# Expert slots walked backwards, and partial tiles filled with the expert's own rows in place of written padding rows

## The chip, the cores and the metric

One core of one Trainium2 chip runs the whole kernel in one launch. The metric is the device time of that execution in microseconds. The kernel before takes 541.59 us (median of 3 runs, 537.69 to 542.88). Engine names are those of the profile: PE (TensorE matmul), PEld (its weight loads), DVE (VectorE), ACT (ScalarE), POOL (GpSimd), SP (SyncE); a "q" behind an engine's name (SPq) marks what its instruction queue does by itself, above all the issue of a DMA.

## The reference

128 images of 64x64 give 16 patches each, 2048 tokens of 192 numbers:

```
h = patches @ W.T + b                                   # 768 -> 192
h = h + attention(layernorm(h))                         # 12 heads, 16 tokens of an image, causal, rotary
x = layernorm(h); t = rmsnorm(x) * norm_scale
g = t @ gate_w.T + gate_b                               # 16 experts
top_vals, top_idx = top_k(g, 4); w = softmax(top_vals)
y_e = swiglu(t @ mlp1_w[e].T + mlp1_b[e]) @ mlp2_w[e].T + mlp2_b[e]   # 192 -> 768 -> 384 -> 192
out = h + x + sum over the 4 chosen experts of w_e * y_e
```

Only the four chosen experts of a token count, so 8192 (token, expert) rows have to be computed. Routing by the reference on its own inputs gives experts 0 to 15 these numbers of rows: 361, 358, 1251, 439, 850, 869, 271, 312, 448, 426, 436, 688, 708, 72, 644, 59. In tiles of 128 rows that is 3, 3, 10, 4, 7, 7, 3, 3, 4, 4, 4, 6, 6, 1, 6 and 1: 72 tiles.

## The kernel before, in words

**Stage one** handles 16 tiles of 128 tokens in a software pipeline of seven steps: embedding, attention, norms, gate, top 4, and the place of each chosen row in the DRAM table `routed`. Each expert owns a region of `routed`; `scatter` (L1133) sends a tile's rows with four indirect DMAs from POOL, one for each choice. A routed row (`packet`, 212 numbers) holds the token's 192 values, its 16 weights and its token number. `add_bias` (L982) completes the residual `base`, which SP stores to `out` (`store_base`, L359).

**Between the stages** three things have to be ready. (a) Padding: `pad_regions` (L316) writes, for each expert, 128 rows of zeros (with a token number below the output) behind the expert's last row, 8 experts from SP, 6 from ACT and 2 from POOL; it knows where from `fill_i` (L1004), which exists only once the last tile is counted. (b) The slot table: 16 small DVE steps, each of which waits for the one before (`then_wait`, L1037), give for each of the 79 slots its expert, its first row in `routed`, and the scatter it must wait for (`owed`); PE turns three columns (L557) and DVE copies them to `table_i` (L1070). (c) All 64 scatters have landed. SP waits for all of it (L384 to L389) before it loads the first tile of rows (L396).

**Stage two** runs 79 slots, the most that 16 experts can need; slot j is one tile of one expert. PE, ACT and DVE take slots in pairs: PE turns the rows (L574), multiplies by the first layer (L594, L602), later by the second (L616); ACT copies weights (L639), applies silu (L730) and notes the row weight (L747); DVE adds the bias, clips, multiplies (L1077, L1082, L1090), and `weigh` (L1093) multiplies by the row weight into one of NY = 4 buffers `y_out` (L1097), where it waits for the scatter of slot j-4. POOL adds the tile to `out` with an indirect DMA that accumulates (L1196). Two such DMAs may touch the same token if they belong to different experts. So POOL always waits for scatter j-2 (L1187), and for scatter j-1 (L1194) where the table says so: where slot j is the first tile of an expert, and for every slot past the last used tile. Those spare slots read a region of padding rows and compute like any other. In the kernel before, the used tiles are slots 0 to 71 in the order of the experts, and the spare ones are slots 72 to 78.

The changed lines, whole:

Of the kernel before, what the change touches and what calls it, by code (L numbers as in the profile page):

```python
# [16 lines left out]
P = 128  # L17
# [23 lines left out]
PAD_SPLIT = (0, 8, 14, 16)  # L41
TABLE_STEPS = 16
# [18 lines left out]
for _name, _n in (("ident", P), ("cos", HD), ("sin", HD), ("head", HH), ("odd", 2), ("own", 2), ("causal", SEQ),  # L61
                  ("expert", EXPERTS), ("region", EXPERTS), ("grow", EXPERTS), ("tile", 1), ("pad", 1),
                  ("before", P), ("token", TILES), ("owed", 1)):
    C_COLS[_name] = (_at, _at + _n)
    _at += _n
# [3 lines left out]
def shape_constants():  # L69
# [3 lines left out]
    def put(name, value):  # L73
        a, b = C_COLS[name]
        c[:, a:b] = value
# [22 lines left out]
def build(nc, x, consts, w_tok, b_tok, w_qkv, b_qkv, w_proj, nscale, w_gate, b_gate,  # L98
          w1, b1, w2, b2, out):
    routed = nc.dram_tensor("routed_rows", (SPARE + P, ROW), F32, kind="Internal").ap()  # L100
    with ExitStack() as ctx:
# [33 lines left out]
        pad_row = sb("pad_row", [P, ROW])  # L135
# [44 lines left out]
        cnt = sb("cnt", [P, EXPERTS])  # L180
        cnt_i, cnt_i2 = sb("cnt_i", [P, EXPERTS], I32), sb("cnt_i2", [P, EXPERTS], I32)
        fill_i = sb("fill_i", [1, EXPERTS], I32)
        ntile, tend = sb("ntile", [P, EXPERTS]), sb("tend", [P, EXPERTS])
        passed, jump, jumped = sb("passed", [P, EXPERTS]), sb("jump", [P, EXPERTS]), sb("jumped", [P, EXPERTS])
        of_tile = sb("of_tile", [P, 6])
        passed_n = sb("passed_n", [P, EXPERTS])
# [15 lines left out]
        row_w = sb("row_w", [P, NX])  # L202

# [10 lines left out]
        def turned(b, a, rows=HALF):  # L214
# [10 lines left out]
        ps_tab = banks[3][0:1, 0:3 * SLOTS]  # L225
# [11 lines left out]
        setup_pool, setup_dve, setup_act, pad_done = sem("setup_pool"), sem("setup_dve"), sem("setup_act"), sem("pad_done")  # L237
# [13 lines left out]
        counted, table_step, fill_ready, table_turned, table_ready, spare_out = (  # L251
            sem(n) for n in ("counted", "table_step", "fill_ready", "table_turned", "table_ready", "spare_out"))
        pads_out = [sem(f"pads_out{i}") for i in range(3)]
# [3 lines left out]
                   "experts_done y_out_ready").split()  # L257
# [58 lines left out]
        def pad_regions(eng, i):  # L316

            eng.wait_ge(fill_ready, 1)
            with eng.Fori(PAD_SPLIT[i], PAD_SPLIT[i + 1] - 1, 2) as e0:
                for u in range(2):  # L320
                    at = eng.value_load(fill_i[0:1, bass.ds(e0 + u, 1)], min_val=0, max_val=SPARE - P)  # L321
                    eng.dma_start(routed[bass.ds(at, P), :], pad_row[:]).then_inc(pads_out[i], 16)  # L322

# [4 lines left out]
        def _(sp):  # L328
# [47 lines left out]
            sp.wait_ge(pad_done, 1)  # L376
            sp.dma_start(routed[SPARE:SPARE + P, :], pad_row[:]).then_inc(spare_out, 16)
            sp.dma_start(out[TOKENS:TOKENS + P, :], pad_row[:, 0:DIM]).then_inc(dump_out, 16)
# [5 lines left out]
            sp.wait_ge(spare_out, 16)  # L384
            for i in range(3):
                sp.wait_ge(pads_out[i], 16 * (PAD_SPLIT[i + 1] - PAD_SPLIT[i]))
# [24 lines left out]
        def _(pe):  # L411
# [142 lines left out]
            pe.wait_ge(s["base_full"], TILES)  # L554
            pe.wait_ge(table_step, TABLE_STEPS)
            for i in range(3):
                last = mm(ps_tab[:, i * SLOTS:(i + 1) * SLOTS], of_tile[0:SLOTS, i:i + 1], ident[0:SLOTS, 0:SLOTS],  # L557
                          start=True, stop=True)
            last.then_inc(table_turned, 1)
# [6 lines left out]
            pe.wait_ge(s["base_full"], TILES)  # L566
            pe.wait_ge(s["row_i_ready"], TILES)
# [69 lines left out]
        def _(act):  # L637
# [78 lines left out]
            pad_regions(act, 1)  # L716
# [54 lines left out]
        def _(dve):  # L771
# [6 lines left out]
            V.tensor_copy(pad_row[:, ID_AT:ID_AT + 1].bitcast(I32), const("pad")).then_inc(pad_done, 1)  # L778
# [183 lines left out]
            def place_all(t):  # L962
                dve.wait_ge(s["ranked"], t + 1)
                V.tensor_tensor(place[:], ps_r, const("region"), ALU.add).then_inc(s["place_ready"], 1)
# [23 lines left out]
            def step(tile, seen, n):  # L988
# [12 lines left out]
                if isinstance(tile(6), int) and tile(6) == TILES - 1:  # L1001

                    dve.wait_ge(counted, 1)
                    V.tensor_tensor(fill_i[:], ps_cnt[0:1, :], const("region", 1), ALU.add).then_inc(fill_ready, 1)  # L1004
# [25 lines left out]
                at(6, add_bias)  # L1030
# [6 lines left out]
            def then_wait(instruction):  # L1037

                instruction.then_inc(table_step, 1)
                made[0] += 1  # L1040
                dve.wait_ge(table_step, made[0])


            then_wait(V.tensor_scalar(cnt_i[:], ps_cnt, float(P - 1), None, ALU.add))
            then_wait(V.tensor_scalar(cnt_i2[:], cnt_i[:], P.bit_length() - 1, None, ALU.logical_shift_right))
            then_wait(V.tensor_copy(ntile[:], cnt_i2[:]))
            then_wait(V.tensor_tensor_scan(tend[:], ones_f[:], ntile[:], 0.0, ALU.mult, ALU.add))

            then_wait(V.tensor_scalar(jump[:], ntile[:], -float(P), float(REGION), ALU.mult, ALU.add))

            then_wait(V.tensor_scalar(passed[:], tend[:], const("tile"), None, ALU.is_le))
            then_wait(V.tensor_tensor(jumped[:], passed[:], jump[:], ALU.mult))
            then_wait(V.tensor_reduce(of_tile[:, 2:3], passed[:], AX_X, ALU.add))
# [201 lines left out]
```

## Time and profile before

| | |
|---|---|
| median of 3 runs | 541.59 us (537.69 to 542.88) |
| profiled execution | 542.0 us, span 540.2 us |
| PE / ACT / DVE / POOL busy | 440.9 / 310.8 / 298.8 / 256.9 us |
| chain that ended last, by engine | PE 57%, issue 9%, DVE 9%, ACT 6%, DMA 4%, SPq 4%, POOL 4% |
| L594 PE, first layer, 948 matmuls | 124.0 us |
| L616 PE, second layer, 474 matmuls | 83.9 us |
| L1196 POOL, 25 of the 79 accumulating scatters | 40.1 us, 1605 ns each |
| L1140 POOL, 64 scatters into `routed` | 63.5 us, 992 ns each |

The span has three parts. Stage one fills it up to some 220 us, then there is a stretch in which PE hardly works, then stage two. Shares of busy time over the whole span mix these, so the rows further down are read stretch by stretch. A timeline row gives start, duration, engine, line, operation and, in brackets, how long the engine had been idle before and what released it; a group such as "x8" spans from its first to its last member.

### The profile page before, as it was taken

Reading aid. Unit: us, or ns where it says so; the run is one execution under the profiler, and the core shown is the slowest. Engines: PE = TensorE matmul, PEld = TensorE weight load, DVE = VectorE, ACT = ScalarE, POOL = GpSimd, SP = SyncE. Lnnn points to the kernel's source line nnn. Section 1 sums busy time; section 2 is a strip of 40 time slices with the busy share of each in tenths; the row PEclk is TensorE's granted clock in tenths of the full one; section 3 lists DMA queues with packets and bytes.
Section 4 is the critical chain, followed back from the end, with each engine's and each line's share of the span. In section 5 each row is a group of like instructions: output and inputs, shape, how many; then the busy total and the mean of one; then the engine's idle time right before and its main releaser. Section 6 shows DMA issues by size and latency. Waiting matters only on the chain.

```text
span 540.2 us, 14340 instructions
## 1 busy us (share of the span) xinstructions
PE 440.9 (82%) x3865; PEld 390.1 (72%) x3866; DVE 298.8 (55%) x964; ACT 310.8 (58%) x832; POOL 256.9 (48%) x303
## 2 busy tenths in 40 slices
PE   2888977878787767119999999999999999999910
PEld 2676756556665545108999999999999999999910
DVE  0467968878778665403555555555555555555510
ACT  1247656666556642016777777777777777777600
POOL 1114576667677556700346444444444444444332
PEclk9789999999997755558999999999999999999965
DMA  8965454565541111333234444444344444432211
GB/s 222 257 158 166 138 152 147 172 172 153 153 134 51 41 41 56 128 114 101 52 55 78 61 63 61 63 61 61 53 69 61 61 61 62 63 40 30 24 22 22
DMA packets 41914, 49.72 MB, mean 92 GB/s; under 512 B 6387, under 2 KB 33251, under 8 KB 41860
## 3 DMA queue, kind: packets, MB, share of 16 engines
q1 hardware_dynamic: 26452, 33.48, 23.1%
q0 software_dynamic: 14544, 14.94, 17.9%
q10 hardware_dynamic: 864, 0.65, 0.4%
q8 instruction: 25, 0.41, 0.3%
q14 instruction: 29, 0.24, 0.2%
HBM read 30.82 MB, written 18.23 MB: 91 GB/s over the span
## 4 chain that ended last, share of the span: by engine, by line
PE 57%; issue 9%; DVE 9%; ACT 6%; another core or an unknown queue 5%; DMA 4%; SPq 4%; POOL 4%; POOLq 1%; DVEq 0%; ACTq 0%
PE bank L594 21%; PE bank L616 14%; PE bank L602 11%; PE bank L574 3%; PE bank L422 2%; ACT k_spread L657 2%; ACT p_spread L639 2%; POOL routed_rows L1140 2%; DMA out_rows<-x_sb 1%; SPq L322 1%; DMA x_sb<-patches 1%; SPq L321 1%; DVE t_row L902 1%; POOL rstd L1131 1%
## 5 line engine op out<-in xcount | busy, mean ns | idle before, releaser
L594 PE MATMUL bank<-rT,w_now 128*128 128x128 f32 x948 | 124.0, 281 | 0.3 <-ACT rT L639 0.3
L594 PEld LDWEIGHTS bank<-rT,w_now 128*128 128x128 f32 x948 | 115.1, 193 | 5.2 <-ACT rT L639 0.5
L730 ACT ACTIVATE k_spread<-bank,w_now 128x128 f32<-128x128 f32 x237 | 69.9, 372 | 58.1 <-PE bank L602 58.1
L1077 DVE TENSOR_TENSOR v_sb<-bank,w_now 128x384 f32<-128x384 f32 x79 | 44.1, 558 | 101.4 <-PE bank L602 80.4
L639 ACT ACTIVATE w_now<-w_sb 128x1158 f32 x79 | 92.5, 1171 | 13.4 <-issue 7.9
L616 PE MATMUL bank<-w_sb,p_spread 128*128 x474 | 83.9, 327 | 0.1
L1196 POOL DMA_INDIRECT out_rows<-x_sb,wtok_sb x25 | 40.1, 1605 | 79.9 <-issue 33.0
L616 PEld LDWEIGHTS bank<-w_sb,p_spread 128*128 128x128 f32 x474 | 76.1, 190 | 0.5 <-issue 0.4
L1140 POOL DMA_INDIRECT routed_rows<-packet,row_i x64 | 63.5, 992 | 24.2 <-issue 22.5
L602 PE MATMUL bank<-rT,w_now 64*128 64x128 f32 x948 | 64.2, 282 | 0.0
L1090 DVE SCALAR_TENSOR_TENSOR p_spread<-k_spread,v_sb 128x384 f32<-128x384 f32 x79 | 44.2, 560 | 35.7 <-ACT k_spread L730 31.4
L602 PEld LDWEIGHTS bank<-rT,w_now 64*128 64x128 f32 x948 | 56.4, 188 | 5.0 <-issue 0.2
L422 PE MATMUL bank<-wtok_sb,x_sb 128*128 128x192 f32 x192 | 38.5, 356 | 10.0 <-DMA wtok_sb<-w_tok 5.7
L422 PEld LDWEIGHTS bank<-wtok_sb,x_sb 128*128 128x128 f32 x192 | 36.0, 212 | 10.0 <-DMA wtok_sb<-w_tok 5.3
L657 ACT ACTIVATE k_spread<-bank,cst 96x256 f32<-96x256 f32 x96 | 36.4, 480 | 0.0
L639 ACT ACTIVATE p_spread<-pT 32x384 f32<-32x384 f32 x64 | 33.2, 518 | 2.6 <-DVE pT L872 2.0
L639 ACT ACTIVATE rT<-bank 128x256 f32<-128x256 f32 x79 | 26.2, 381 | 13.7 <-PE bank L574 13.0
L1097 DVE TENSOR_SCALAR x_sb<-bank,row_w 128x192 f32<-128x192 f32 x79 | 29.2, 410 | 5.4 <-DMA out_rows<-x_sb,rope_s 3.9
L639 ACT ACTIVATE yT<-bank 128x384 f32<-128x384 f32 x16 | 7.8, 490 | 40.1 <-remote 37.3
L1082 DVE TENSOR_SCALAR v_sb<-v_sb 128x384 f32<-128x384 f32 x79 | 29.2, 369 | 2.7
L467 PE MATMUL bank<-wproj_sb,yT 128*128 128x192 f32 x96 | 23.1, 386 | 8.1 <-issue 4.4
L1128 POOL TENSOR_SCALAR ve<-mv 128x1 f32<-128x1 f32 x32 | 7.2, 225 | 44.2 <-DVE mv L802 36.1
(174 smaller groups left out, 688.6 us busy)
## 6 DMA issues: line engine op xcount, KB each, us to landing
x_sb<-patches SPq DMA_DIRECT2D x16, 384.0 KB, 3.4
w_sb<-w SPq DMA_DIRECT2D x32, 192.0 KB
w_sb<-w SPq DMA_DIRECT2D x16, 288.0 KB
w_sb<-w SPq DMA_DIRECT2D x64, 48.0 KB
wtok_sb<-routed_rows SPq DMA_DIRECT2D x25, 106.0 KB, 2.0
out_rows<-h SPq DMA_DIRECT2D x16, 96.0 KB
wproj_sb<-routed_rows SPq DMA_DIRECT2D x10, 106.0 KB
x_sb<-routed_rows SPq DMA_DIRECT2D x10, 106.0 KB
```

What stands on the lines that cost most here:

```text
L422: last = mm(ps_e, x_sb[buf][:, c, :], wtok_sb[:, c, :], start=(c == 0), stop=(c == PCH - 1))
L594: last = mm(dst[:, c * P:(c + 1) * P], w[:, a:a + P], t[:, part, :], start=(start and c == 0), stop=(not start and c == ICH - 1))
L602: last = mm(dst[:, c * P:(c + 1) * P], w[k:k + half, REST + c * P:REST + (c + 1) * P], t[k:k + half, 1 - part, :], start=(start and c == 0 ...
L616: last = mm(ps_yo[buf % 2], act_sb[buf % 4][:, c, :], w2_sb[:, bass.ds(expert, 1), c, :].rearrange("p a f -> p (a f)"), start=(c == 0), st ...
L639: return nc.scalar.activation(dst, src, ACT.Copy)
L657: last = nc.scalar.activation(k_spread[:, :, :, h], ps_kT.rearrange("p c (j i k) -> p c j i k", j=PAIRS, i=2), ACT.Copy, scale=const("head ...
L730: last = nc.scalar.activation(gate_act[b][:, a:a + P], ps_glu[b][:, a:a + P], ACT.Silu, bias=w1_now[b][:, GLU_B + c:GLU_B + c + 1], scale= ...
L1077: V.tensor_tensor(lin[b].rearrange("p (c t) -> p c t", c=ICH), ps_lin[b][:, 0:INNER].rearrange("p (c t) -> p c t", c=ICH), w1_now[b][:, LI ...
L1082: V.tensor_scalar(lin[b], lin[b], 1.0 + LIMIT, 1.0 - LIMIT, ALU.min, ALU.max).then_inc(r["clip_ready"], 1)
L1090: V.scalar_tensor_tensor(act_sb[buf % 4].rearrange("p c t -> p (c t)"), gate_act[b], SILU_LIMIT, lin[b], ALU.min, ALU.mult).then_inc(r["ac ...
L1140: G.indirect_dma_start(out=routed, out_offset=bass.IndirectOffsetOnAxis(ap=row_i[buf][:, k:k + 1].bitcast(U32), axis=0), in_=packet[buf][: ...
L1196: G.indirect_dma_start(out=out, out_offset=bass.IndirectOffsetOnAxis(ap=rows[b][:, ID_AT:ID_AT + 1].bitcast(U32), axis=0), in_=y_out[b % N ...
```

## The change

Slot j now takes tile 78-j of the old order: `tile` becomes 78 minus the slot, so the spare slots are 0 to 6 and the last slots are the tiles of expert 0. Within an expert too the last tile comes first. No padding is written behind an expert's rows. A slot whose tile is partial starts at (last row - 127) and so reads the last 128 rows of its expert; the rows that a neighbouring slot owns too are computed twice, and their results are sent to the 128 rows below the output. For that each region begins with 128 rows of zeros (needed by an expert with fewer than 128 rows), written by SP ahead of the routing's end: 17 DMAs. In stage two DVE makes the list of target rows (`row_to`) for each slot with one more instruction on 128x1 elements, POOL waits for it, and the scatter uses it. `owed` is set where a slot is its expert's last tile, and for spare slots. The table needs 22 steps where 16 stood, each of which waits only for the step it reads; the last `add_bias` runs behind them; a fourth matmul and one DVE instruction make `pad_to`, the list of double rows.

```
-PAD_SPLIT = (0, 8, 14, 16)
-TABLE_STEPS = 16
+TABLE_STEPS = 22
...
-    put("region", np.arange(EXPERTS)[None, :] * REGION)
+    put("region", np.arange(EXPERTS)[None, :] * REGION + P)
-    put("tile", p[:, None])
+    put("tile", SLOTS - 1 - p[:, None])
+    put("next", SLOTS - p[:, None])
+    put("past", -P * (SLOTS - 1 - p[:, None]))
+    put("row", P - p[:, None])
...
-        def pad_regions(eng, i):
-            eng.wait_ge(fill_ready, 1)
-            with eng.Fori(PAD_SPLIT[i], PAD_SPLIT[i + 1] - 1, 2) as e0:
...
-            sp.wait_ge(pad_done, 1)
-            sp.dma_start(routed[SPARE:SPARE + P, :], pad_row[:]).then_inc(spare_out, 16)
+            sp.wait_ge(setup_pool, 3)
+            sp.dma_start(out[TOKENS:TOKENS + P, :], zero_row[:, 0:DIM]).then_inc(dump_out, 16)
+            for e in range(EXPERTS + 1):
+                sp.dma_start(routed[e * REGION:e * REGION + P, :], zero_row[:]).then_inc(heads_out, 16)
-            with sp.Fori(TILES - 8, TILES - 1) as t:
+            with sp.Fori(TILES - 8, TILES) as t:
                 store_base(t)
-            pad_regions(sp, 0)
-            store_base(TILES - 1)
+            sp.wait_ge(heads_out, 16 * (EXPERTS + 1))
...
+            mm(ps_valid, of_tile[0:SLOTS, 3:4].to_broadcast([SLOTS, P]), ident[0:SLOTS, 0:SLOTS],
+               start=True, stop=True).then_inc(table_turned, 1)
+            pe.wait_ge(pad_to_ready, 1)
+            pe.wait_ge(setup_dve, 4)
...
-            pad_regions(act, 1)
...
+            tab(10, V.tensor_reduce, column[7], ends_at[:], AX_X, ALU.max)
+            tab(15, V.scalar_tensor_tensor, column[3], column[6], cnt[:, 0:1], const("past"), ALU.add, ALU.add)
+            tab(16, V.tensor_tensor, column[9], column[7], passed[:, EXPERTS - 1:EXPERTS], ALU.max)
+            tab(19, V.scalar_tensor_tensor, column[1], column[3], float(P), column[8], ALU.min, ALU.add)
+            tab(20, V.scalar_tensor_tensor, column[2], column[9], 16.0, const("owed"), ALU.mult, ALU.add)
+            add_bias(TILES - 1)
+            dve.wait_ge(table_turned, 1)
+            V.tensor_copy(table_i[:].rearrange("p a j -> p (a j)"), ps_tab).then_inc(table_ready, 1)
+            V.tensor_scalar(pad_to[:], ps_valid, const("row"), const("pad"), ALU.is_lt, ALU.mult)
...
             def weigh(j, buf):
+                V.scalar_tensor_tensor(row_to[:, buf % NY:buf % NY + 1], rows[buf][:, ID_AT:ID_AT + 1].bitcast(I32),
+                                       float(TOKENS - 1), pad_to[:, bass.ds(j, 1)], ALU.min, ALU.max)
...
-            pad_regions(pool, 2)
...
+                    pool.wait_ge(r["row_to_ready"], j + 1)
-                        ap=rows[b][:, ID_AT:ID_AT + 1].bitcast(U32), axis=0),
+                        ap=row_to[:, b % NY:b % NY + 1].bitcast(U32), axis=0),
```

How the change moves instructions shows at two places. First SP, from the store of the zero rows below the output to the first load of routed rows; before:

```order
L377 DMA routed_rows<-pad_row 128x212 [waits pad_done]
L378 DMA out_rows<-pad_row 128x192
L361 DMA out_rows<-h 128x192
...
L319 UNCONDITIONAL_BRANCH [waits fill_ready]
L321 TENSOR_LOAD fill_i
L322 DMA routed_rows<-pad_row 128x212
...
L361 DMA out_rows<-h 128x192 [waits base_full]
L395 TENSOR_LOAD table_i [waits scattered0,scattered1,pads_out2,table_ready,pads_out1,spare_out,pads_out0]
L396 DMA wtok_sb<-routed_rows 128x212
```

and now:

```order
L372 DMA out_rows<-zero_row 128x192 [waits setup_pool]
L374 DMA routed_rows<-zero_row 128x212 x17
L356 ISA [waits base_full]
...
L387 TENSOR_LOAD table_i [waits table_ready,scattered1,heads_out,scattered0]
L388 DMA wtok_sb<-routed_rows 128x212
```

The padding loop behind the last count is gone, and 17 DMAs stand far ahead of it. Second DVE, from the last placing of rows to the table's copy (`cnt_i`, `of_tile` and the like are the table's workings, `w_sb` the first layer's bias columns); before:

```order
L980 CAST row_i<-row_f 128x4 [waits scattered1,row_f_ready]
L986 TENSOR_TENSOR h<-h,bank 128x192 [waits base_ready,b2_done]
L1044 TENSOR_SCALAR cnt_i<-bank 128x16
...
L1063 SCALAR_TENSOR_TENSOR of_tile<-of_tile,cst 128x1 [waits table_step]
L1067 TENSOR_SCALAR w_sb<-bank 128x16x3 [waits b1_turned,table_step]
L1068 TENSOR_SCALAR w_sb<-bank 128x16x3
L1070 CAST table_i<-bank 1x237 [waits table_turned]
```

and now:

```order
L975 CAST row_i<-row_f 128x4 [waits scattered1,row_f_ready]
L1033 TENSOR_SCALAR cnt_i<-bank 128x16 [waits counted]
L1033 COPY cnt<-bank 128x16
...
L1033 SCALAR_TENSOR_TENSOR of_tile<-of_tile,cst 128x1 [waits table_step]
L981 TENSOR_TENSOR h<-h,bank 128x192 [waits base_ready,b2_done]
L1063 CAST table_i<-bank 1x237 [waits table_turned]
L1064 TENSOR_SCALAR pad_to<-bank,cst 128x79
L1068 TENSOR_SCALAR w_sb<-bank 128x16x3 [waits b1_turned]
L1069 TENSOR_SCALAR w_sb<-bank 128x16x3
```

The residual's last addition has moved behind the table's steps, and the bias columns behind the table's copy.

## Rows read from the trace of the kernel before

**Rows 1.** The page: PE's busy tenths in 40 slices of 13.5 us.

```profile
PE   2888977878787767119999999999999999999910
```

**Rows 2.** Timeline between the stages, all engines: start us, us, engine, line, idle before.

```profile
217.50 0.96 POOL L1140 DMA_INDIRECT routed_rows<-packet,row_i  x1 [0.30 <-issue]
...
219.98 0.36 ACT L639 ACTIVATE packet<-t_row 128x192 f32<-128x192 f32 x1 [2.88 <-DMA routed_rows<-packet,row_i]
...
220.92 0.17 DVE L980 CAST row_i<-row_f 128x4 int32<-128x4 f32 x1
...
221.93 0.17 DVE L1044 TENSOR_SCALAR cnt_i<-bank 128x16 int32<-128x16 f32 x1
...
222.84 15.71 SPq L322 DMA_DIRECT2D routed_rows<-pad_row  x8
...
224.53 0.15 DVE L1058 TENSOR_SCALAR of_tile<-of_tile 128x1 f32<-128x1 f32 x1
225.01 0.17 DVE L1059 TENSOR_TENSOR passed_n<-passed,ntile 128x16 f32<-128x16 f32 x1 [0.33 <-issue]
...
227.62 0.96 POOL L1140 DMA_INDIRECT routed_rows<-packet,row_i  x1 [0.30 <-issue]
227.83 0.16 DVE L1063 SCALAR_TENSOR_TENSOR of_tile<-of_tile,cst 128x1 f32<-128x1 f32 x1 [0.48 <-DVE of_tile L1061]
...
229.34 0.95 PE L557 MATMUL bank<-cst,of_tile 79*1 79x79 f32 x6 [7.72 <-DVE of_tile L1063]
...
231.00 0.38 DVE L1070 CAST table_i<-bank 1x237 int32<-1x237 f32 x1
...
242.79 0.66 PE L574 MATMUL bank<-cst,wtok_sb 128*128 128x128 f32 x2 [12.15 <-DMA wtok_sb<-routed_rows]
```

**Rows 3.** Timeline of SP's queue: before stage one ends, and the first row loads.

```profile
154.98 0.43 SPq L378 DMA_DIRECT2D out_rows<-pad_row  x1
161.34 56.52 SPq L361 DMA_DIRECT2D out_rows<-h  x7
...
240.69 3.64 SPq L396 DMA_DIRECT2D wtok_sb<-routed_rows  x4
```

**Rows 4.** The chain that ended last, in order of time: start us, us, what.

```profile
238.22 1.69 DMA routed_rows<-pad_row
...
263.26 1.95 PE bank L616 x12
...
494.46 1.95 PE bank L616 x12
```

**Rows 5.** Timeline of POOL in stage two: its scatters into the output.

```profile
259.64 1.66 POOL L1196 DMA_INDIRECT out_rows<-x_sb,wtok_sb  x1 [29.91 <-DVE x_sb L1097]
...
272.69 1.54 POOL L1196 DMA_INDIRECT out_rows<-x_sb,wtok_sb  x1 [2.77 <-DVE x_sb L1097]
...
301.30 1.56 POOL L1196 DMA_INDIRECT out_rows<-x_sb  x1 [3.79 <-issue]
303.17 1.55 POOL L1196 DMA_INDIRECT out_rows<-x_sb  x1 [0.30 <-issue]
...
506.73 1.72 POOL L1196 DMA_INDIRECT out_rows<-x_sb,p_pair  x1 [2.68 <-DMA out_rows<-x_sb,pT]
511.86 1.55 POOL L1196 DMA_INDIRECT out_rows<-x_sb,rope_c  x1 [3.41 <-DMA out_rows<-x_sb,p_pair]
...
533.00 1.56 POOL L1196 DMA_INDIRECT out_rows<-x_sb,k_spread  x1 [2.59 <-DMA out_rows<-x_sb]
```

**Rows 6.** Timeline of DVE in stage two: a pair in the middle, and the last ones.

```profile
299.17 0.74 DVE L1097 TENSOR_SCALAR x_sb<-bank,row_w 128x192 f32<-128x192 f32 x2
301.55 0.56 DVE L1077 TENSOR_TENSOR v_sb<-bank,w_now 128x384 f32<-128x384 f32 x1 [1.64 <-PE bank L602]
...
503.07 0.73 DVE L1097 TENSOR_SCALAR x_sb<-bank,row_w 128x192 f32<-128x192 f32 x2
...
515.51 0.42 DVE L1097 TENSOR_SCALAR x_sb<-bank,row_w 128x192 f32<-128x192 f32 x1 [1.51 <-PE bank L616]
519.85 0.42 DVE L1097 TENSOR_SCALAR x_sb<-bank,row_w 128x192 f32<-128x192 f32 x1 [3.92 <-DMA out_rows<-x_sb,rope_s]
```

More of the change, by code:

```diff
@@ L61 @@
 for _name, _n in (("ident", P), ("cos", HD), ("sin", HD), ("head", HH), ("odd", 2), ("own", 2), ("causal", SEQ),
-                  ("expert", EXPERTS), ("region", EXPERTS), ("grow", EXPERTS), ("tile", 1), ("pad", 1),
+                  ("expert", EXPERTS), ("region", EXPERTS), ("grow", EXPERTS), ("tile", 1), ("next", 1), ("past", 1), ("row", 1), ("pad", 1),
                   ("before", P), ("token", TILES), ("owed", 1)):
@@ L1029, in step, with tab @@
                 at(1, rope_add)
-                at(6, add_bias)
+                if n < TILES + STAGES - 2:
+                    at(6, add_bias)
             unrolled(STAGES, TILES, step)
             made = [0]
-            def then_wait(instruction):
-                instruction.then_inc(table_step, 1)
+            def tab(needs, op, *args):
+                if needs:
+                    dve.wait_ge(table_step, needs)
+                op(*args).then_inc(table_step, 1)
                 made[0] += 1
-                dve.wait_ge(table_step, made[0])
@@ L1044, in _ @@
[L1044 to L1051, printed above, removed]
@@ L1064, in _ @@
-            assert made[0] == TABLE_STEPS
+            column = [of_tile[:, i:i + 1] for i in range(10)]
+            dve.wait_ge(counted, 1)
+            tab(0, V.tensor_scalar, cnt_i[:], ps_cnt, float(P - 1), None, ALU.add)
+            tab(0, V.tensor_copy, cnt[:, 0:EXPERTS], ps_cnt)
+            tab(1, V.tensor_scalar, cnt_i2[:], cnt_i[:], P.bit_length() - 1, None, ALU.logical_shift_right)
+            tab(2, V.tensor_tensor, fewer[:], cnt[:, 1:EXPERTS + 1], cnt[:, 0:EXPERTS], ALU.subtract)
@@ new lines, in _ @@
+            tab(3, V.tensor_copy, ntile[:], cnt_i2[:])
+            tab(5, V.tensor_tensor_scan, tend[:], ones_f[:], ntile[:], 0.0, ALU.mult, ALU.add)
+            tab(5, V.tensor_scalar, jump[:], ntile[:], -float(P), float(REGION), ALU.mult, ALU.add)
+            tab(5, V.scalar_tensor_tensor, left[:], ntile[:], float(P), fewer[:], ALU.mult, ALU.add)
+            tab(6, V.tensor_scalar, passed[:], tend[:], const("tile"), None, ALU.is_le)
+            tab(6, V.tensor_scalar, ends_at[:], tend[:], const("next"), None, ALU.is_equal)
@@ L1065, in _ @@
+            assert made[0] == TABLE_STEPS
+            add_bias(TILES - 1)
+            dve.wait_ge(table_turned, 1)
+            V.tensor_copy(table_i[:].rearrange("p a j -> p (a j)"), ps_tab).then_inc(table_ready, 1)
+            V.tensor_scalar(pad_to[:], ps_valid, const("row"), const("pad"), ALU.is_lt, ALU.mult
+                            ).then_inc(pad_to_ready, 1)
             dve.wait_ge(b1_turned, 1)
```

70 lines of the change are left out of this document (29 added, 41 removed).

## The prediction, written before the changed kernel ran

> **What bounds the kernel now.** I read the page's busy slices first: PE is busy at 90% or more from slice 20 on, and works at a tenth in slices 17 and 18 [rows 1]. So stage two is PE's, and two stretches are not: the gap between the stages and the end. The timelines of these two and the chain that ended last say what each waits for.
>
> Stage two in its middle: the chain is PE alone, and a pair of slots takes (494.46 - 263.26) / 34 = 6.80 us [rows 4], 3.40 a slot. DVE is idle for 1.64 us before it starts a pair [rows 6]. POOL issues a pair's two scatters at 301.30 and 303.17, 2.13 us after DVE began to weigh the pair at 299.17, and 1.87 apart [rows 5, 6].
>
> The gap: the last scatter into `routed` is issued at 227.62; the table is in place at 231.38 (231.00 + 0.38) [rows 2]. Yet SP issues its first row load at 240.69 [rows 3]. The chain shows why: it passes through a padding DMA that lands at 239.91 (238.22 + 1.69) [rows 4]; SP's eight padding DMAs alone stretch over 15.71 us [rows 2]. PE starts 2.10 us after that load, at 242.79, having been idle for 12.15 us.
>
> The end: the last slot is weighed at 519.85, after 3.92 us of waiting for a free `y_out` buffer, and POOL issues the last six scatters from 511.86 to 533.00, (533.00 - 511.86) / 5 = 4.23 us apart, each released by the landing of the one before [rows 5, 6]. Those are slots 73 to 78, all spare. A chained scatter takes 4.2 us where PE needs 3.4 for the slot, so at the end of the program POOL runs long after PE, for rows that nobody reads.
>
> **The change, part by part.**
>
> *Padding leaves the gap.* SP now waits for the later of two things. The scatters: the last of an earlier tile was issued at 217.50 and released ACT at 219.98, so it lands 2.48 us after its start; the last one of all, started at 227.62, lands at 230.1 [rows 2]. POOL's own queue of scatters sets this, and the change leaves it alone. The table: DVE can start at 221.1, behind the cast at 220.92 (+0.17); `add_bias`, which stood ahead and waited for PE, is behind the table now. The first twelve steps took from 221.93 to 224.68, 0.23 us each; the last four from 225.01 to 227.99, 0.75 each, while padding DMAs were in flight [rows 2]. I have 22 steps: at 0.23 they end at 226.2. With slow steps like those four at 0.75 it is 228.2, and with every step behind 225.0 at 0.75 (five of them) 228.8. Then PE: 1.35 us from step to matmul (227.99 to 229.34), 0.95 for three transposes and a third of that, 0.32, for the fourth, and 0.1 + 0.38 for the copy: 3.1 us, with 0.35 for `add_bias` hidden beside PE. Table in place: 229.3, at worst 231.9. SP's first load came 0.78 us behind the last padding (240.69 against 239.91), so now at 230.9 if the scatters decide and at 232.7 if the worst table does. I take 231.4, half a microsecond above the lower end, since slow steps have been seen once: **9.3 us less**, between 8.0 and 9.8. What would be late next: PE also waits for the bias columns and `pad_to`, three small DVE instructions behind the copy, about 0.9 us; the rows need 2.1 us from issue to PE, so these hide. ACT's table load and first weight copy stood behind its padding loop and now run ahead.
>
> A rule of the Trainium skill ("SBUF — State Buffer", the part on the "DVE blocks DMA" trap) speaks against the longer table: while VectorE runs certain fp32 instructions it locks GpSimd out of the port through which it writes DMA descriptors. By that rule the six added steps, 0.17 us each, could put up to 1.0 us on the last scatter's landing and on the sum. The trace speaks for none: the scatters from 217.50 to 227.62 are (227.62 - 217.50) / 8 = 1.265 us apart, with table steps beside some of them and an idle DVE beside others [rows 2].
>
> *17 zero DMAs from SP.* They follow the store at 154.98, at 0.47 us each: 8 us, to about 163. SP's next job, a store, waited until 161.34 anyway [rows 3], so it slips by some 2 us and nobody waits for it. On the DMA engines they run beside stage one's last expert weights and the scatters of three or four tiles. I cost this at nothing: a packet buffer is reused two tiles later. If that cover were gone, the bound is the padding's own length, some 16 us for 8 on SP with others beside [rows 2]; stage one's 22 pipeline steps in 220 us are 10 us each, so two of them still cover it, and I allow 3 us for what shares the queues beside. A gain has no reason.
>
> *Reversal, the start.* Slots 0 to 6 are spare, 7 is expert 15's only tile, 8 expert 14's last: scatters 1 to 8 are chained. Before, three links at the start took (272.69 - 259.64) / 3 = 4.35 us each [rows 5], and PE's pace did not suffer. Count from the first weighing: scatter 0 at 1.35, scatter 7 at 1.35 + 7 x 4.35 = 31.8; it lands 3.65 later (a buffer was freed at 515.51 by the scatter of 511.86 [rows 5, 6]), at 35.5. Slot 11 needs that buffer and would be weighed at 5 x 6.8 + 0.4 = 34.4. So DVE stands for 1.1 us once, inside the 1.64 us it idles in each pair. From slot 9 on most slots are unchained and the backlog goes. Cost 0; with links of 4.7 it would be about 2.
>
> *One more DVE instruction and wait for each slot.* A 128x1 instruction takes 0.15 us (L1058), with its wait at most 0.5 [rows 2]. Two in a pair are 0.3, at most 1.0, within 1.64: 0.
>
> *Reversal, the end.* The last slots are expert 1's tiles (73, 74, 75) and expert 0's (76, 77, 78); chained are 73 and 76. With the pair of slots 72 and 73 weighed at 503.07 as now (before the shift), scatter 72 goes at 505.2 (+2.13), 73 one link later at 509.4, 75 needs 73 landed: 513.5, 76 is chained to 75: 517.7, 77 follows by 1.87, and 78 needs 76: 521.9 (four links of 4.17 to 4.23). PE is done at 515.5 and hides. Before it was 533.00, so **11.1 us less**; with links of 4.35, 10.4; if the links shrink to 4.1, 11.5. What follows the last scatter (540.2 - 533.0 = 7.2 us) stays.
>
> **Sum**: 542.0 - 9.3 - 11.1 = 521.6 us against the profiled execution; that lies 0.4 above the median of the runs shown, so I say 521.5.
>
> **The rivals.**
>
> *The table takes the padding's place.* If its steps are slow for a reason other than the padding (DVE's instructions arriving late, say), all 22 at 0.75 end at 237.6 and the copy at 240.7: nothing is won in the gap. For it: the slow steps began at 225, four microseconds after the first padding. Against: padding was in flight when they came, and twelve steps ran at 0.23. Time 542.0 - 11.1 = 531. Chance 0.09.
>
> *The start's chain reaches PE.* If links are 5 us with row loads and weights beside them (one at the end was 5.1, from 506.73 to 511.86 [rows 5]), slot 11's weighing comes some 6 us late; 1.6 of it is DVE's idle time, and PE's double buffers take some more: 3 to 5 us lost, 525 to 527. Against: 4.35 in just that place. Chance 0.07.
>
> *Slower: the owed column chains every slot.* The new test marks a slot where an expert's end equals the slot's tile number plus one. If it marked all slots, stage two would run at POOL's link: scatter 78 at 250.3 + 78 x 4.23 = 580, end near 587. It decides from about 60% of slots chained: with 4.23 for a chained slot and half of that for the others, which wait for the scatter two back, the mean passes PE's 3.4 a slot there. Against: the constants give 16 experts' ends and 7 spare slots. The same side is reached if `row_to` made a pair over 2.3 us longer for DVE (its 1.64 us of slack, and 25 us / 39.5 pairs more), over seven times 0.3. Together 0.02.
>
> *It doesn't do what it says at the end:* spare slots leave the end but another wait keeps POOL there, a saving of the gap alone: 533. Against: the rules of rows 5. Chance 0.03.
>
> The forecast itself has 0.79: 516 to 527.
>
> **Range and chances.** Bounds of the gap (8.0 to 9.8) and end (10.4 to 11.5) give 521 to 523.5, the zero DMAs up to 3 more. The runs before spread over 5 us, and so does a median of new ones in part: 515 to 528 with the start's chain in it; up to 530 toward the table's rival. 515 to 530. A change under 1%, 5.4 us, can't be told from none here: faster than 536.2 takes all cases but the slower one and what I can't name, 0.94; within 1% 0.03; slower 0.03.
>
> **What would show it.** Right: SP's first row load near 231 and no DMA from `pad_row` between; the first landing wait named for it a scatter into `routed`, or the table; PE idle 3 us, not 12; the last POOL scatter about 11 us closer to PE's last matmul, 6 or 7 behind it; eight POOL links over 4 us at the start of stage two; PE's pair still at 6.80 us. Wrong: table steps at 0.7 us throughout, a DVE wait for `out_rows` longer than 2 us in the first six pairs, PE steps in stage two over 6.9, or stage one ending later than 228 us with ACT or DVE waiting for `packet`.

## The result, and the profile after

The changed kernel takes 522.23 us (median of 4 runs, 521.43 to 525.02); the kernel before took 541.57 us beside it. The ratio is 0.9664, with a 95% interval of 0.9603 to 0.9724: faster by 19.3 us. The profiled execution took 521.43 us.

The page has a span of 519.6 us; PE's busy tenths in slices of 13.0 us:

```profile
PE   3788887797777758339999999999999999999970
```

Against [rows 1], slices 17 and 18, the stretch between the stages, stand at 3 tenths where they stood at 1, and slice 39 is busy at 7 tenths where it stood at 1.

The stretch between the stages, timeline of all engines:

```profile
218.88 0.17 DVE L975 CAST row_i<-row_f 128x4 int32<-128x4 f32 x1
...
221.49 0.15 DVE L1033 TENSOR_SCALAR of_tile<-of_tile 128x1 f32<-128x1 f32 x1 [0.45 <-DVE of_tile L1033]
...
222.96 0.16 DVE L1033 SCALAR_TENSOR_TENSOR of_tile<-of_tile 128x1 f32<-128x1 f32 x1 [0.60 <-DVE of_tile L1033]
...
225.59 0.96 POOL L1144 DMA_INDIRECT routed_rows<-packet,row_i  x1 [0.31 <-issue]
...
226.79 0.40 DVE L1063 CAST table_i<-bank 1x237 int32<-1x237 f32 x1 [3.27 <-issue]
...
229.10 4.76 SPq L388 DMA_DIRECT2D wtok_sb<-routed_rows  x5
```

SP loads the first rows 10.22 us after the last cast of `row_i`, where it was 19.77 [rows 2, 3]. The table is in place at 227.19, 1.9 us before that load; the last scatter, issued at 225.59, lands about 228.1 by the 2.48 us of [rows 2]. So the scatters set the start, and the table is ready only 0.9 us before they land. PE is idle for 4.2 us before its first slot (226.91 to 231.12), where the prediction said 3 and the kernel before had 12.15.

The end, POOL's last scatters (slots 73 to 78), then DVE's weighing of slots 74 and 78, of the timeline:

```profile
497.60 1.90 POOL L1200 DMA_INDIRECT out_rows<-x_sb,row_to  x1 [2.71 <-DMA out_rows<-x_sb,row_to]
499.82 1.64 POOL L1200 DMA_INDIRECT out_rows<-x_sb,row_to  x1 [0.32 <-issue]
503.19 1.56 POOL L1200 DMA_INDIRECT out_rows<-x_sb,row_to  x1 [1.73 <-DMA out_rows<-x_sb,row_to]
507.44 1.56 POOL L1200 DMA_INDIRECT out_rows<-x_sb,row_to  x1 [2.68 <-DMA out_rows<-x_sb,row_to]
509.30 1.56 POOL L1200 DMA_INDIRECT out_rows<-x_sb,row_to  x1 [0.30 <-issue]
512.43 1.56 POOL L1200 DMA_INDIRECT out_rows<-x_sb,row_to  x1 [1.57 <-DMA out_rows<-x_sb,row_to]
```

```profile
498.05 0.41 DVE L1100 TENSOR_SCALAR x_sb<-bank,row_w 128x192 f32<-128x192 f32 x1
...
503.97 0.41 DVE L1100 TENSOR_SCALAR x_sb<-bank,row_w 128x192 f32<-128x192 f32 x1
```

From the weighing of slots 74 and 75 to the last scatter it is 14.38 us (498.05 to 512.43), where it was 23.4. No weighing waits for a scatter now; the last one comes at 503.97.

The span's 20.6 us split at three marks. Stage one up to the `row_i` cast: 220.92 against 218.88, 2.0. Cast to first row load: 9.55. First row load to the last scatter: 292.31 against 283.33, 9.0, all of it behind the weighing of slot 74. The 7.2 us behind the last scatter are the same.

### The profile page after: what moved, and what is told of

Read it like the earlier page. It is cut to its first block and busy times, and to the rows that moved or that the text cites. A ratio compares the mean times of both kernels' runs of the same rounds, so it can differ in the third digit from the quotient of the medians.

```text
span 519.6 us, 14443 instructions
## 1 busy us (share of the span) xinstructions
PE 437.7 (84%) x3867; PEld 388.2 (75%) x3868; DVE 303.9 (58%) x1048; ACT 311.0 (60%) x832; POOL 257.2 (50%) x302
## 5 line engine op out<-in xcount | busy, mean ns | idle before, releaser
L1200 POOL DMA_INDIRECT out_rows<-x_sb,row_to x79 | 125.9, 1593 | 161.6 <-DMA out_rows<-x_sb,row_to 78.5
L1144 POOL DMA_INDIRECT routed_rows<-packet,row_i x64 | 64.7, 1012 | 24.1 <-issue 22.2
L1100 DVE TENSOR_SCALAR x_sb<-bank,row_w 128x192 f32<-128x192 f32 x79 | 31.8, 410 | 0.0
L459 PEld LDWEIGHTS bank<-wproj_sb,yT 128*128 128x128 f32 x96 | 18.5, 224 | 12.7 <-issue 12.7
```

The lines of the kernel that those rows point to most:

```text
L459: last = mm(ps_p, yT[:, c, :], wproj_sb[:, c, :], start=(c == 0), stop=(c == YCH - 1))
L1144: G.indirect_dma_start(out=routed, out_offset=bass.IndirectOffsetOnAxis(ap=row_i[buf][:, k:k + 1].bitcast(U32), axis=0), in_=packet[buf][: ...
L1200: G.indirect_dma_start(out=out, out_offset=bass.IndirectOffsetOnAxis(ap=row_to[:, b % NY:b % NY + 1].bitcast(U32), axis=0), in_=y_out[b % ...
```

## Experiments

Each kernel is the changed one with the edit shown, or the kernel before where its heading says so. "Gap" is the time from the last `row_i` cast to SP's first row load, "tail" that from the weighing of slots 74 and 75 to the last scatter, both from the run's profile; times are medians, each beside runs of the kernel before on the same chip. The experiments ran on three chips, 0, 8 and 13, which matters: on chip 0 the kernel before takes 524 us, on chips 8 and 13 it takes 543 and 544. Headings say where a chip comes in first.

**Repeated, unaltered** (chip 0).

> The changed kernel once more, unaltered, to see what belongs to the change and what to the execution. The two profiles split the 20.6 us of span into 2.0 in stage one (up to the last tile's row_i cast), 9.6 between that cast and PE's first work of stage two, 0.0 in stage two up to the weighing of slots 74 and 75, and 9.0 from there to the last scatter. My theory (stage one's 2.0 us are chance) expects the first part to be anywhere from 217 to 222 us and the other three within 0.3 us of 12.2, 266.9 and 14.5. A rival (the change itself shortens stage one) expects 218.9 again and again, and 220.9 in kernels with padding writes.

Measured: 512.70 us against 524.25, ratio 0.979 (0.9766 to 0.9814). Gap 10.30, tail 14.48, as expected; but stage one ends at 206.87, 12 us earlier than in the first profile and outside my 217 to 222. All four profiles of changed kernels on this chip end stage one between 206.87 and 211.33, all those on the other chips between 218.50 and 223.37, so that part goes with the chip. And the change is worth 11.5 us here, not 19.3: something in it is worth less.

**Old order of the slots.**

```
+    put("tile", p[:, None])
+    put("next", p[:, None])
+    put("past", -P * p[:, None])
```

> The changed kernel with the slots in the old order (spare slots last, tiles ascending, a slot chained where it is its expert's first tile); no padding, row_to as in the changed kernel. My theory (the tail is a chain of scatters of spare slots): the gap stays 12.2 us, the last scatter goes 23.4 us after the weighing of slots 74 and 75 and not 14.5, time 522.2 + 9.0 = 531.2, ratio to before 0.981. Rival (the tail was shortened by something else, for example row_to or the missing padding traffic): time near 522. Rival (the start's chain of eight costs PE something): less than 531, since that chain is gone too.

Measured: 522.73 us, ratio 0.997 (0.9939 to 1.0001), gap 10.32, tail 23.26. The reversal is worth 10.0 us by the medians. In the profiles the tail has 8.8 of it (23.26 against 14.48), and from the first row load to the weighing of slots 74 and 75 the two kernels take the same to 0.1 us, so the start's chain costs nothing that could be seen. The expected ratio was missed, since almost nothing was left to all other parts of the change: 1.5 us, with an interval that includes none.

**Padding put back.**

```
+            pad_regions(sp, 0)
...
+            pad_regions(act, 1)
...
+                    V.tensor_tensor(fill_i[:], ps_cnt[0:1, :], const("region", 1), ALU.add).then_inc(fill_ready, 1)
...
+            pad_regions(pool, 2)
```

> The changed kernel with the 16 padding DMAs put back where they stood (8 from SP, 6 from ACT, 2 from POOL, behind the count of the last tile; nobody reads the rows), reversed order kept. My theory (the gap waited for the padding): from the row_i cast to PE's first work 21.9 us and not 12.2, the end as in the changed kernel; time 522.2 + 9.6 = 531.8. Rival (the table's shorter dependencies made the gap shorter): time near 522 to 525.

Measured: 514.42 us, ratio 0.9819 (0.9797 to 0.984), gap 12.31, tail 14.07. The theory's size fell: the gap grows by 2.0 us, not by 9.6, and the time by 1.7. The rival's small cost (0 to 3 us) is what this chip shows, but not for the rival's reason: the table is in place at 214.43, and in the chain that ended last the first row load at 222.03 stands behind SP's last padding DMA, issued at 218.80. So padding does set the gap here too, at a fifth of the price. With the tail's 8.8 the 2.0 make up 10.8 of the 11.5 us that the change is worth on this chip.

**The owed count is loaded ahead of POOL's waits.**

```
+                        owed = pool.value_load(table_i[0:1, 2, bass.ds(j, 1)], ...)
                     pool.wait_ge(r["row_to_ready"], j + 1)
...
-                        owed = pool.value_load(table_i[0:1, 2, bass.ds(j, 1)], ...)
                         pool.wait_ge(added[(b - 1) % 2], owed)
```

> In the changed kernel POOL reads the owed count of a slot before it waits for the slot's data and for scatter j-2, not after. My prediction took 4.2 us for every link at the end; the profile shows 5.0 (507.44 to 512.43) and 5.6 where the link is the wait for scatter j-2, and 4.3 where it is the table's. My theory: the table's value is loaded behind the j-2 wait and costs 0.8 us there. Then this kernel has links of 4.2 to 4.3 in both cases, its even scatters go 1.1 to 1.3 us after the weighing and not 1.8 to 2.1, and the end comes 2.0 to 2.5 us earlier: 520. Rival (the j-2 links are long because two scatters in flight slow each other's landing): 522, links of 5 us stay.

Measured: 511.04 us, ratio 0.9737 (0.972 to 0.9755), below the changed kernel's interval on the same chip; tail 12.56. POOL's scatters of slots 73, 75, 76 and 78 here, and then those of the unaltered repeat:

```profile
490.21 1.55 POOL L1202 DMA_INDIRECT out_rows<-x_sb,row_to  x1 [2.73 <-DMA out_rows<-x_sb,row_to]
...
494.88 1.70 POOL L1202 DMA_INDIRECT out_rows<-x_sb,row_to  x1 [0.87 <-issue]
499.35 1.56 POOL L1202 DMA_INDIRECT out_rows<-x_sb,row_to  x1 [2.77 <-DMA out_rows<-x_sb,row_to]
...
503.79 1.56 POOL L1202 DMA_INDIRECT out_rows<-x_sb,row_to  x1 [1.02 <-DMA out_rows<-x_sb,row_to]
```

```profile
486.06 1.90 POOL L1200 DMA_INDIRECT out_rows<-x_sb,row_to  x1 [2.72 <-DMA out_rows<-x_sb,row_to]
...
491.71 1.56 POOL L1200 DMA_INDIRECT out_rows<-x_sb,row_to  x1 [1.79 <-DMA out_rows<-x_sb,row_to]
496.08 1.56 POOL L1200 DMA_INDIRECT out_rows<-x_sb,row_to  x1 [2.81 <-DMA out_rows<-x_sb,row_to]
...
500.99 1.56 POOL L1200 DMA_INDIRECT out_rows<-x_sb,row_to  x1 [1.49 <-issue]
```

Slot 73 to 75 falls from 5.65 to 4.67 us, 76 to 78 from 4.91 to 4.44, and slot 72's scatter goes 1.23 us after its weighing, no longer 1.77; the chained link 75 to 76 is 4.47 against 4.37. Together, 0.98 + 0.47 + 0.54 - 0.10, that is the tail's 1.9 us. So the load behind the wait cost 0.5 to 1.0 us a link; the theory had 0.8. What keeps these links at 4.4 to 4.7 us, where it expected 4.2 to 4.3, is not shown; the rival (two scatters in flight slow each other) may have that rest.

**The kernel before, repeated** (chip 8).

> The kernel before once more, unaltered, for a profile under the conditions of the experiments: there the changed kernel took 512.7 us and the one before 524.25, each 10 to 17 us less than in the first runs, and only 11.5 apart. With padding put back into the changed kernel the time rose by 1.7 us, where 9.6 were expected. My theory now: in the first profiles something held up the instruction supply of the engines (SP's plain register instructions took up to 0.7 us in the padding loop, PE finished steps of stage one late), so padding took 18 us there and takes less here, while the end of the program, a chain of DMAs, is the same. It expects: row_i cast to SP's first row load 12 to 13.5 us (19.8 in the first profile, 12.3 with padding back), the last six scatters 4.2 us apart, 23 us from the weighing of slots 74 and 75 to the last scatter. Rival (the padding costs as much here, and the kernel with padding back hides it in some way): 18 us or more to the first row load.

Measured: 542.79 us against 542.67, gap 19.90, tail 24.01. The expectation assumed the conditions of chip 0, and this chip is like that of the first profiles: the test didn't decide between theory and rival, but it repeats the first profile's gap to 0.13 us. SP's padding and first load:

```profile
222.91 15.69 SPq L322 DMA_DIRECT2D routed_rows<-pad_row  x8
...
240.83 4.76 SPq L396 DMA_DIRECT2D wtok_sb<-routed_rows  x5
```

**Every slot chained.**

```
-            tab(16, V.tensor_tensor, column[9], column[7], passed[:, EXPERTS - 1:EXPERTS], ALU.max)
+            tab(16, V.tensor_tensor, column[9], ones_f[:, 0:1], passed[:, EXPERTS - 1:EXPERTS], ALU.max)
```

> The changed kernel with the owed column set so that every slot's scatter waits for the one before. My theory: stage two then runs at the chained link and no longer at PE's pace: 78 links of 4.27 us, so 333 us from the first scatter to the last where the changed kernel has 264.4; time 512.7 + 69 = 582. PE then waits for DVE and DVE for a free y_out. Rival (links shorten when fewer row loads compete): 4.1 us and 568.

Measured: 595.13 us in one run, beside 542.67 before. The first scatter goes at 248.15, the last at 586.15: 338.0 us for 78 links, 4.33 each. Of the 13 us between the expected time and this, some 9.5 are the chip's (522.2 against 512.7 for the changed kernel) and 5 the links' (338 against 333); so the expected 333 was 1.5% low. The link's price holds over the whole stage; a kernel that chained all slots would be 52 us slower than the one before.

**Twelve more dependent steps ahead of the table's last.**

```
+            for i in range(12):
+                tab(made[0], V.tensor_copy, late_col[:], column[9])
```

> The changed kernel with 12 more dependent DVE instructions (a copy of one column, result unused) ahead of the table's last step, 12 x 0.2 = 2.4 us. In the repeated run of the changed kernel the table is in place at 211.56 and the last scatter into routed lands near 216.1, so the scatters set the start of the row loads with 4.6 us to spare. My theory: cast to first row load stays at 10.3 us. Rival (SP's wait for the table decides, or the longer DVE work delays POOL's descriptors): 12.7 us, or scatters more than 1.27 us apart.

Measured: 526.64 us in one run, gap 13.39. Here the table does decide. Part of DVE's timeline, with SP's first load:

```profile
225.09 0.16 DVE L1034 SCALAR_TENSOR_TENSOR of_tile<-of_tile 128x1 f32<-128x1 f32 x1 [1.24 <-DVE of_tile L1034]
226.49 0.91 DVE L1034 COPY late_col<-of_tile 128x1 f32<-128x1 f32 x5 [1.24 <-DVE of_tile L1034]
227.89 0.15 DVE L1034 COPY late_col<-of_tile 128x1 f32<-128x1 f32 x1 [0.49 <-DVE late_col L1034]
228.59 0.91 DVE L1034 COPY late_col<-of_tile 128x1 f32<-128x1 f32 x5 [0.55 <-DVE late_col L1034]
229.99 0.15 DVE L1034 COPY late_col<-of_tile 128x1 f32<-128x1 f32 x1 [0.49 <-DVE late_col L1034]
...
232.11 0.39 DVE L1066 CAST table_i<-bank 1x237 int32<-1x237 f32 x1 [1.51 <-PE bank L552]
```

```profile
233.66 4.76 SPq L389 DMA_DIRECT2D wtok_sb<-routed_rows  x5
```

Against the first profile of the changed kernel the table's copy is 3.93 us later behind the cast (11.84 against 7.91) and the first load 3.17 (13.39 against 10.22): the table had 0.8 us to spare, not the 4.6 of chip 0. Equal copies run in groups of five, one, five and one, 0.19 us apart, and stand still in between; every restart lies one or two times 0.70 us from the last: 225.09, 226.49, 227.89, 228.59, 229.99. The last scatter into `routed` is issued 6.80 us after the cast, against 6.71 with a shorter table. So the part of the rival on SP's wait for the table came true, and the part on POOL's descriptors did not show.

**24 empty instructions at the start of DVE's program.**

```
+            for _ in range(24):
+                alone(dve)
```

> The changed kernel with 24 empty instructions at the start of DVE's program, where DVE waits for its first input anyway. In the first profile the table's last eight steps were slow (idle 0.45, 0.36 and 0.60 us), though no padding was in flight; in the repeated run they were not. If instructions that arrive late are the cause and this shows under these conditions at all, the slow place moves by 24 instructions to the front; if nothing is slow here either, the table takes 3.2 to 3.5 us from first to last step as before, and the time stays within 1% of 512.7. Rival (the slow steps belong to those instructions): they come back in the same place.

Measured: 522.27 us in one run, gap 10.72. The steps are slow here too, at other places than in the first profile:

```profile
222.14 0.17 DVE L1035 TENSOR_REDUCE of_tile<-lefts 128x1 f32<-128x16 f32 x1 [0.54 <-DVE of_tile L1035]
...
222.86 0.22 DVE L1035 SCALAR_TENSOR_TENSOR of_tile<-of_tile,cnt,cst 128x1 f32<-128x1 f32 x1 [0.35 <-DVE of_tile L1035]
223.56 0.16 DVE L1035 TENSOR_TENSOR of_tile<-of_tile,passed 128x1 f32<-128x1 f32 x1 [0.48 <-DVE of_tile L1035]
225.69 0.16 DVE L1035 SCALAR_TENSOR_TENSOR of_tile<-of_tile 128x1 f32<-128x1 f32 x1 [1.96 <-remote]
```

The first idle place of 0.4 us or more moved from step 17 to step 15, not by 24 steps, so the simple form of my theory is wrong; but it isn't these instructions' own cost either, since the step that waited 0.45 us in the first profile is not slow here. The 0.70 us grid is here as well (222.14, 222.86, 223.56). What decides the place is open.

**Padding put back, again** (chip 13).

> The changed kernel with the 16 padding DMAs put back, as in the run that cost only 1.7 us. Runs have fallen under two conditions: in one (kernel before 542, changed 522) instructions come late in steps of 0.70 us, in the other (524 and 512.7) they don't. My theory (the padding loops, with two register loads and a back branch for each two DMAs, are slowed by late instructions, so the padding costs 9.6 us in the first condition and about 2 in the second): ratio of this kernel to the one before 0.980 to 0.984 in both, cast to first row load 19 to 20 us beside a kernel before of 542, and 12.3 beside one of 524. Rival (it is the kernel and not the condition): 12.3 in both.

Measured: 532.90 us against 544.23, ratio 0.9781 (0.9738 to 0.9824), a little below the expected 0.980 to 0.984; gap 20.26, 10.0 us above the 10.22 of the first profile without padding. The same program has a gap of 12.31 us on one chip and of 20.26 on another. SP's side of it, first on chip 0, then here: the register instructions of the padding loop (duration in ns, min/median/max), and the timeline.

```profile
L329 SPq FUSED_REGOPS  x8: 37/37/48, 208.5 to 218.7; - x8
L329 SPq MOVE routed_rows<-zero_row x8: 29/29/29, 208.6 to 218.7; - x8
```

```profile
L329 SPq FUSED_REGOPS  x8: 18/37/700, 223.6 to 239.8; - x8
L329 SPq MOVE routed_rows<-zero_row x8: 7/29/722, 224.3 to 239.9; - x8
```

```profile
208.66 10.47 SPq L329 DMA_DIRECT2D routed_rows<-zero_row  x8
...
222.03 5.16 SPq L404 DMA_DIRECT2D wtok_sb<-routed_rows  x5
```

```profile
225.04 15.25 SPq L329 DMA_DIRECT2D routed_rows<-zero_row  x8
...
242.56 5.16 SPq L404 DMA_DIRECT2D wtok_sb<-routed_rows  x5
```

Instructions that only move a register mostly take 29 to 37 ns, but some take 0.70 to 0.72 us here and none does on chip 0. Eight DMAs stretch over 15.25 us here, 10.47 there, and start 2.7 us after the cast here, 1.1 us before it there: these two differences, 4.8 and 3.8 us, cover the 7.95 us between the gaps. Even on chip 0, where nothing is late, a round of the loop takes 1.45 us: (10.47 - 0.33) / 7, of which SP's load of a register from `fill_i` has 0.48 in the median and the issue of the DMA 0.33.

**The kernel before, a third profile.**

> The kernel before, for its profile beside the other three. My theory: if the kernel before takes 524 here, cast to first row load is 11.5 to 13 us; if it takes 542, 19.9 as in both earlier profiles, and SP's eight padding DMAs stretch over 15.7 us again. In both, 23.4 to 24.0 us from the weighing of slots 74 and 75 to the last scatter. Rival (the tail differs between the conditions as well): less than 22 or more than 25.

Measured: 542.86 us in one run, gap 20.20, tail 24.28, eight padding DMAs over 15.27 us. The tail is 0.3 above the bound I gave. There is no profile of the kernel before on chip 0, so its gap there is not known.

**The owed count ahead of the waits, again.**

> The changed kernel with POOL's load of the owed count ahead of its waits, again. In the first run it was 1.7 us faster than the changed kernel's median and the last scatter came 12.6 us after the weighing of slots 74 and 75, not 14.5. My theory (1.9 us at the end, independent of the instruction supply): ratio to the kernel before lower than the changed kernel's by 0.003 to 0.004: 0.9625 beside a kernel before of 542 (520.5 us), 0.974 beside one of 524. Rival (chance between kernels of one call): 0.966 and 0.979.

Measured: 523.89 us, ratio 0.9622 (0.9574 to 0.967), tail 12.58, gap 11.09 with the table's copy at 9.55 behind the cast. Here the table decides, though nothing in DVE's program was changed: it is in place at 231.64 and SP's first load follows 1.15 us later, as it did in the kernel with twelve more steps (1.16). The tail's 1.9 us are there again; the ratio is where the theory put it, though its interval overlaps the changed kernel's.

**Padding as plain DMAs.** The edit is shown against the looped form.

```
-            with eng.Fori(PAD_SPLIT[i], PAD_SPLIT[i + 1] - 1, 2) as e0:
-                for u in range(2):
-                    at = eng.value_load(fill_i[0:1, bass.ds(e0 + u, 1)], min_val=0, max_val=SPARE - P)
-                    eng.dma_start(routed[bass.ds(at, P), :], zero_row[:]).then_inc(pads_out[i], 16)
+            for e in range(PAD_SPLIT[i], PAD_SPLIT[i + 1]):
+                eng.dma_start(spill[e * P:e * P + P, :], zero_row[:]).then_inc(pads_out[i], 16)
```

> The changed kernel with 16 padding DMAs of the same size, on the same three queues behind the same count, but to fixed rows of a table of their own, written out one by one: no register load, no register arithmetic and no loop around them. It tells the DMAs' own time from that of the instructions around them. My theory: SP's eight take 0.4 to 0.6 us each and the padding is over before the last scatter lands; cast to first row load 10.3 us, time within 1 us of the changed kernel in either condition. Rival (the DMA engines or their writes are what took 18 us): with padding in loops and without, the first row load comes equally late.

Measured: 528.57 us, ratio 0.9708 (0.9667 to 0.975), gap 13.18. SP's DMAs, DVE's table copy and the first load:

```profile
221.01 5.09 SPq L328 DMA_DIRECT2D spill_rows<-zero_row  x8
...
235.02 0.39 DVE L1082 CAST table_i<-bank 1x237 int32<-1x237 f32 x1 [1.66 <-PE bank L566]
```

```profile
236.55 5.16 SPq L403 DMA_DIRECT2D wtok_sb<-routed_rows  x5
```

The same bytes on the same queues take SP 5.09 us and not 15.25, and SP's last is issued 9 us before the table is there (POOL's two go behind its last scatter, at 231.1 and 231.7, 4 us before it). So most of the 15 us was the instructions around the DMAs, not the DMAs; the destination is another here too (rows of a table that no scatter writes to), which was not tested apart. The time is 4.3 us below that of the looped form on the same chip, the gap 7.1 us. It isn't back at the changed kernel's gap, as I had expected, since the table's copy comes 11.65 us after the cast here (7.91 in the first profile) and has taken over. The looped form has its copy as late, at 11.95, while the changed kernels without padding and with 22 steps have it at 7.91 to 9.55 (four profiles). On chip 0 it makes no difference: 4.30 without padding, 4.31 with it. So where instructions are late, padding in flight may make DVE's come later still; DVE's program differs too (it computes `fill_i`), and no run tells the two apart.

## Why the prediction was right, step by step

**Padding leaves the gap: 9.3 us forecast, 9.55 measured.** The mechanism and the size held under the conditions of the profile that it was read from. That the padding was what SP waited for is shown by putting it back: the gap is 20.26 us with it on chip 13. But the size is not the kernel's alone: on chip 0 the padding costs 1.7 to 2.0 us (512.70 against 514.42, gap 10.30 against 12.31). The prediction took the 15.71 us of [rows 2] for the padding's own length. Written out plainly, the same eight DMAs take 5.09.

**The table: 229.3 at the earliest, 0.8 us before the scatters' landing, forecast.** It came 0.9 us before, but for a partly wrong reason. I put the slow steps of [rows 2] down to padding in flight as the likelier cause; without any padding slow steps were there again (0.45, 0.36 and 0.60 us of idle time), so padding is not needed for them, and the doubt in my first rival (instructions that arrive late) was right. Whether padding adds to them is open, as said above. On chip 0 all 22 steps run in 2.4 us. The rival itself, at 0.75 us a step for all of them, didn't come; in its weaker form, a table that decides, it did in three experiments: twelve more steps, plain padding, and the owed count loaded early on chip 13. With 0.8 us to spare, that the table was no limit in the first profile is partly luck.

**The rule on descriptors that VectorE holds up** (the Trainium skill, "SBUF — State Buffer") would have put up to 1.0 us on the last scatter. With six more table steps, and with 18 more, the last scatter goes 6.71 and 6.80 us after the cast, as before (6.70, 227.62 - 220.92). Twelve of the 18 are copies of 128x1 numbers, and they run beside that scatter (226.49 to 230.14, the scatter from 227.07). No run here shows the lock with these small instructions; the landing of that scatter is hidden behind the table.

**The end: 11.1 us forecast, 9.0 measured.** Right in kind, 2.1 us too large. The mis-sized term is the link between a scatter and the one two slots on: I took 4.17 to 4.23 us, that of a chained pair. POOL loads the owed count behind that wait, and the link is 5.59 us from slot 73 to 75 and 4.99 from 76 to 78. From scatter 72 to 78 that makes 19.1 us (493.29 to 512.43) where I had 16.7, and scatter 72 went 0.4 us earlier behind its weighing than forecast. Moving the load ahead took 1.9 us off the tail, twice.

**The start's chain: 0 forecast, 0 measured.** The forecast's 3.65 us from a scatter to a free buffer came from a row that names PE and not the scatter (515.51 in [rows 6]); slot 78's weighing, which does name it, gives 3.67 (516.18 to 519.85). Scatters 0 and 8, and the moment in which slot 11 was weighed:

```profile
248.04 1.61 POOL L1200 DMA_INDIRECT out_rows<-x_sb,row_to  x1 [21.49 <-DVE x_sb L1100]
...
282.23 1.56 POOL L1200 DMA_INDIRECT out_rows<-x_sb,row_to  x1 [2.63 <-DVE x_sb L1100]
```

```profile
281.56 0.16 DVE L1097 SCALAR_TENSOR_TENSOR row_to<-qk,pad_to 128x1 int32<-128x1 int32 x1 [0.42 <-issue]
...
283.15 0.56 DVE L1077 TENSOR_TENSOR v_sb<-bank,w_now 128x384 f32<-128x384 f32 x1 [1.11 <-PE bank L597]
```

Eight links take 34.2 us, 4.27 each (4.35 forecast), and slot 11 waits 0.4 us where 1.1 was forecast; DVE still idles 1.11 us behind it for PE, so PE was not held up.

**`row_to`: 0.** It takes 0.15 us, hidden, and PE's pair of slots stays at 6.80 us: (489.48 - 251.48) / 35.

```profile
251.48 2.12 PE L611 MATMUL bank<-w_sb,p_spread 128*128 x12
...
489.48 2.12 PE L611 MATMUL bank<-w_sb,p_spread 128*128 x12
```

**The 17 zero DMAs: 0 forecast.** They took SP from 152.39 to 162.16, 9.8 us where the forecast had 8, and stage one was no longer: 218.88 against 220.92. Those 2.0 us I hadn't forecast. Other profiles of changed kernels on such chips end stage one at 218.50, 220.27, 219.41, 222.30, 221.70 and 223.37, those of the kernel before at 220.93 and 220.42: the two ranges overlap, so I read the 2.0 as chance, unproved.

The sum came within 0.7 us (521.5 against 522.23) by luck in part: the tail's 2.1 too much met the 2.0 of stage one. And it holds on chips like the one it was read from; on chip 0 the same change is worth 11.5 us.

## What to carry to other kernels

A price read from one profile belongs to its conditions: before calling a stretch of DMAs slow, look at the durations of the plain register instructions beside them, and at the same stretch on another chip. Padding whose place is known only after the last count falls into the stretch in which little else runs: looped, it cost 2.0 us of gap on one chip and 10 on another. Written out plainly it cost less, and an overlapping full tile that is read in its place does without it. Put work that nobody needs at the start of a chained queue, where other engines' work covers it, and not at its end, and load the count to wait for before the waits: that version is the fastest here, 511.04 us where the changed kernel takes 512.70.

## What the runs showed of the hardware

- Late instructions. On two chips, and on the one of the first profiles, the profile names "remote" (by its chain: another core or an unknown queue) as what stage one waited for, and on chip 0 that row does not appear. Waits up to 222 us in the first profile of the changed kernel (in total, times, longest):

```profile
ACT yT L634 <- remote: 36.4, 12, 4.4
```

  Together with the 0.70 us grid on DVE and SP it comes with a kernel that takes 542 to 544 us instead of 524. That it is instructions that arrive late is the reading that fits, not one that a run proves. The profile's page has DMA queues of the kind "instruction", and they moved the same on both sides (25 and 30 packets in the changed kernel, on chip 0 as in the first profile), so nothing more was fetched where it was slow. The Trainium skill ("Runtime: NRT & Kernel Launch", Instruction fetch mechanics) says that each engine's sequencer fetches its instructions by DMA, and that taken branches break the fetching ahead. The instruction queues of the profile agree with the first; the wait for a fetch is not seen in any row. That the looped padding took 15.25 us and the plain one 5.09 fits the part on branches, but the loads of a register went with the loop, so the two are not told apart. Why chips differ is open.
- A scatter of 128 rows that accumulates in DRAM and is chained to the one before takes 4.27 to 4.33 us from start to start, over 8 links and over 78.
